# Attended values kept by feature, three score banks in turn, and the causal triangle added by VectorE in a fused attention and MoE kernel

## Chip, cores and metric

The kernel runs on one core of a Trainium2 chip. The metric is device time in microseconds for one execution. TensorE is the matrix engine (PE in the rows), VectorE is DVE, ScalarE is ACT, GpSimd is POOL, SyncE is SP.

## What is computed

```
xn  = layernorm(x)                       # x: 2 x 1024 x 512, float32
Q, K, V = xn @ Wq.T, xn @ Wk.T, xn @ Wv.T   # 16 heads of 32 features
S   = where(causal, Q K^T / sqrt(32), -1e30)
O   = softmax(S) @ V
att = O.reshape(b, t, D) @ Wo.T
ffn = sum over the top 2 of 8 experts (grouped sigmoid routing) of w * expert(xn)
      + shared(xn)                       # both are silu(x g^T) * (x u^T) d^T
out = x + att + ffn
```

Every large product is made in pieces: an operand is split into a rounded part (`_hi`) and a remainder (`_lo`), and the products of the parts are summed, so that float32 accuracy is kept with the fast `fp32r` matmul.

## The kernel before

Five phases follow each other, with a barrier between: norm, project (Q, K), attend, out (the Wo product and the residual), routed (the experts). The change touches attend and out.

**Attend.** 32 heads (16 heads by 2 batches), each in 12 steps; a step is one block of up to 128 keys by 512 queries. All five engines walk the same list of steps, each in its own order, and every stage has a lag in steps. On TensorE, in step s: `score(s-24)` (L1458), the piece of a second product for `maximum(s)` (L1432) that finds each row's maximum two heads ahead, `value(s-30)` (two matmuls, L1481 and L1483, that sum the 66 by 512 output of a head's half in `ps_o`), and between them `shared(s)`: so many matmuls of the shared expert (L1514, L1539) as the planner `fill_counts` gives that step. There are 864 of those, spread so that each step has the same planned cost (`step_cost`). Eight of a head's twelve blocks lie on the diagonal; there `score` adds the triangle of -1e30 with one more matmul, identity by `late` (L1463). Twice in a head `turn_o` turns the 66 by 512 output into rows with four transposes (L1494), after ScalarE has copied it (`o_copy`, L1252).

VectorE: `maximum` reduces each piece from one of two banks (L1306, L1310; L1314 joins two halves), `lo` for two of twelve blocks, `normalize` copies the turned output from PSUM (L1336), `weigh_o` takes the reciprocals of 128x4 sums (L1350), adds the two halves (L1352) and multiplies (L1356). The shared expert's `gate`, `hidden`, `hidden_lo` and `add` run on it too. ScalarE: `exp` from the score bank into one of four `prob` slots (L1236), then `hi` (L1243), the copies and the tanh. GpSimd: `lo` for ten of twelve blocks (L1198), and in between the steps of `place`, the list of routed rows, which ends in 32 indirect DMAs (L1166), one in each step. The order is copy, exp, row, hi on ScalarE. `ps_s` has two banks; `ps_x` is a bank shared by the turned output and by the turned row of maxima. SP issues loads head by head: six loads of Q and K, the values, and, at set heads, `load_xt`, `load_base`, `store_acc` and the raw weights of the second shared expert (`load_gate_up`, L1019), which ScalarE splits in `split_shared` (L1277).

**Out.** For each of 16 row tiles: VectorE copies the tile (L1651), TensorE turns it with four transposes (L1684), ScalarE and VectorE split it (L1636, L1657), TensorE multiplies by Wo in 12 matmuls (L1697), VectorE adds (L1665).

Of the kernel before, what the change touches and what calls it, by code (L numbers as in the profile page):

```python
# [33 lines left out]
P = 128  # L34
# [15 lines left out]
HEAD_SLOTS = 4  # L50
W_SLOTS = 4
# [39 lines left out]
def moe_attention_kernel(nc, x, wqk, wv, wo, router, bias, gate, up, down, sgate, sup, sdown, out):  # L91
# [5 lines left out]
    slots_dram = nc.dram_tensor("slots", [NSLOT, 2], F32, kind="Internal").ap()  # L97
    xt_dram = nc.dram_tensor("xt_blocks", [NTB, P, 2, KC, TBW], F32, kind="Internal").ap()
    with ExitStack() as ctx:
# [29 lines left out]
        with ExitStack() as shared_ctx:  # L129
# [25 lines left out]
            attend_phase(nc, x, ident, qk_hi, qk_lo, qs, ks, head_loaded, v_dram, row_dram, xt_dram,  # L155
# [25 lines left out]

def load_head(eng, g, qk_hi, qk_lo, qs, ks, head_loaded):

    c, h, b = g % HEAD_SLOTS, g // B, g % B
# [9 lines left out]
def wait_head_stored(eng, g, qk_stored):  # L194
    h, n = g // B, len(qk_stored)
# [583 lines left out]
def attend_phase(nc, x, ident, qk_hi, qk_lo, qs, ks, head_loaded, v_dram, row_dram, xt_dram, xt,  # L779
# [22 lines left out]
    COPY, TURN, NORM = VALUE + 1, VALUE + 2, VALUE + 3  # L802
    ROW = NB + 2
    DEEPEST = NORM
# [26 lines left out]
    def step_cost(s):  # L831
# [37 lines left out]

    def head_after(step):  # L870
        return max(0, -(-(step - (AHEAD + NB - 1) + 1) // NB) + HS)

    XT_AT = [None] + [head_after(step_of(unit - 1, UP_END[-1] - 1)) for unit in range(1, UNITS)]
    ACC_AT = [1] + [head_after(step_of(unit - 1, PER_UNIT - 1) + 1) for unit in range(1, UNITS)]
    RAW_AT = [2] + [head_after(min(SPLIT_AT, key=lambda s: SPLIT_AT[s] != [k - 1]) + 1)
                    for k in range(1, NF)]
    DOWN_RAW_AT = [3, 4, 5]

    with ExitStack() as ctx:
        sbuf, psum, sem = allocator(nc, ctx)  # L880
        vs = sbuf("vs", [P, HS, QT, VW], F32R)
        late = sbuf("late", [P, P], F32R)
        eye = sbuf("eye", [P, P], F32R)
# [9 lines left out]
        o_part = sbuf("o_part", [P, 4, VW])  # L893
        o_sum = sbuf("o_sum", [P, 4, DK])
        o_inv = sbuf("o_inv", [P, 4, 1])
# [17 lines left out]
        slot = sbuf("slot", [P, NT, E])  # L913
        pick = sbuf("pick", [P, NT, E])
# [4 lines left out]
        NS = 2  # L919
        ps_s = [psum(f"ps_s{n}", [P, TBW]) for n in range(NS)]  # L920
        ps_o = psum("ps_o", [P, TBW])
        ps_x = psum("ps_x", [P, TBW])
        ps_ot = ps_x[:, 0:4 * VW].rearrange("p (q w) -> p q w", q=4)
        ps_row = ps_x[:, TBW - P:]
        ps_f = [psum(f"ps_f{n}", [P, TBW]) for n in range(2)]

        values_loaded = [sem(f"values_loaded{n}") for n in range(HS)]
# [9 lines left out]
        s_done = sem("s_done")  # L937
        exp_done = sem("exp_done")
# [5 lines left out]
        o_turned = sem("o_turned")  # L944
        o_read = sem("o_read")
# [31 lines left out]
        with nc.Block() as block:  # L977
            @block.sync
            def _(sp):
# [6 lines left out]
                def load_values(g):  # L986
                    c, h, b = g % HS, g // B, g % B
                    wait(sp, pv_done, NB * (g - HS + 1))
                    sp.dma_start(vs[:, c, :, 0:2 * DK].bitcast(F32),
                                 v_dram[:, b * QT:(b + 1) * QT, h, :]).then_inc(values_loaded[c], 16)  # L990

# [34 lines left out]
                for g in range(HEADS + 4):  # L1026
                    if HS <= g < HEADS:
                        next_head(g)
                    if g == HEADS // 2:
# [4 lines left out]
                    for unit in range(UNITS):  # L1034
                        if g == XT_AT[unit]:
                            load_xt(unit)
                        if unit and g == ACC_AT[unit]:
                            store_acc(unit - 1)
                        if g == ACC_AT[unit]:
                            load_base(unit)  # L1040
                    if 0 < g <= HEADS:
                        load_values(g - 1)
                    for k in range(NF):
                        if g == RAW_AT[k]:
                            load_gate_up(k)
                        if g == DOWN_RAW_AT[k]:
                            load_shared_down(k)
                store_acc(UNITS - 1)
# [4 lines left out]
            def _(pool):  # L1053
# [23 lines left out]
                def place():  # L1077
# [86 lines left out]
                    for t in range(NT):  # L1164
                        for k in range(2):
# [14 lines left out]
                scratch = prob[:, 0, 0:P]  # L1180
                nc.gpsimd.memset(scratch, 0.0).then_inc(consts_zeroed, 1)
                pool.wait_ge(consts_zeroed, 2)
                nc.gpsimd.affine_select(out=scratch, in_=scratch, compare_op=ALU.is_ge,
                                        fill=MASKED, base=0, pattern=[[1, P]],
                                        channel_multiplier=-1).then_inc(consts_zeroed, 1)
                pool.wait_ge(consts_zeroed, 3)
                nc.gpsimd.tensor_copy(late[:, :], scratch).then_inc(consts_ready, 1)
                nc.gpsimd.tensor_copy(eye[:, :], ident[:, :]).then_inc(consts_ready, 1)
# [107 lines left out]
            def _(dve):  # L1296
# [32 lines left out]
                def normalize(s):  # L1329
                    if s % NB not in ENDS:  # L1330
                        return
# [643 lines left out]
```

## Time and profile before

| what | us |
|---|---|
| median of three runs (lowest, highest) | 1119.6 (1117.81, 1122.33) |
| the profiled execution's own time | 1127.01 |
| its span, first to last instruction | 1125.0 |
| norm and project | 0 to 184 |
| attend | 184 to 760.5 |
| out | 760.5 to 820.5 |
| routed | 820.5 to 1125 |
| busy, share of the span: TensorE, VectorE, ScalarE, GpSimd | 93%, 70%, 57%, 45% |
| VectorE's four operations on the turned output (L1336, L1350, L1352, L1356), busy in all | 27.1 + 10.8 + 41.1 + 33.2 = 112.2 |

A busy figure is an average over stages with different limits. The clock column is the TensorE clock granted, 1.00 for full speed (2.4 GHz), 0.5 for half (1.2 GHz). Matmuls are pipelined: a 512-column matmul is shown with some 0.4 us, while the next may start 0.23 us after it, so the distance between two starts is the cost, not the duration.

### The profile page before, as it was taken

The numbers are of one execution on the slowest core, as the hardware profiler recorded it, in microseconds if no ns is written. First come the engines' busy times: TensorE is split into PE (matmuls) and PEld (weight loads), VectorE is DVE, ScalarE is ACT, GpSimd is POOL, SyncE is SP. The second block draws the span as 40 slices with busy tenths as digits, with TensorE's granted clock in tenths as the row PEclk, the third lists the DMA queues.
The fourth block names the chain that finished last, engine by engine and source line by source line (L and its number), as shares of the span: only waits on it lengthen the run. The fifth ranks groups of instructions, "written<-read, shape, count | busy, mean of one in ns | idle before, by whom it ended". The sixth has DMA issues, their size and how long they took to land. (4 is left out here: it accounts for less than half of the span.)

```text
span 1125.0 us, 18890 instructions
## 1 busy us (share of the span) xinstructions
PE 1046.2 (93%) x5379; PEld 817.6 (73%) x5380; DVE 784.6 (70%) x1675; ACT 637.9 (57%) x1278; POOL 506.4 (45%) x568
## 2 busy tenths in 40 slices
PE   6999979888899998999999999998989999999994
PEld 4767867666677776777778777776867777778872
DVE  6732324565688887788888888865568888888872
ACT  3323211265588786787787887872155555565550
POOL 0013903388756564556566565651013443333321
PEclk9999989988899999999999999998989999999997
DMA  6989996255543553644445426118789444443432
GB/s 213 322 335 361 136 293 231 94 67 102 132 133 77 150 148 75 163 118 136 115 113 151 126 64 191 45 39 266 243 283 278 90 76 75 75 72 68 71 54 35
DMA packets 106201, 163.61 MB, mean 145 GB/s; under 512 B 53984, under 2 KB 64480, under 8 KB 102656
## 3 DMA queue, kind: packets, MB, share of 16 engines
q1 hardware_dynamic: 95776, 141.82, 44.1%
q0 software_dynamic: 9760, 20.49, 10.0%
q8 instruction: 38, 0.62, 0.2%
q14 instruction: 51, 0.42, 0.1%
q10 hardware_dynamic: 576, 0.26, 0.1%
HBM read 101.25 MB, written 61.28 MB: 144 GB/s over the span
## 5 line engine op out<-in xcount | busy, mean ns | idle before, releaser
L1198 POOL TENSOR_TENSOR prob_lo<-prob,prob_hi 128x512 fp32r<-128x512 f32 (+2 forms) x320 | 308.3, 977 | 203.3 <-ACT prob_hi L1243 147.0
L1236 ACT ACTIVATE prob<-ps_s 128x512 f32<-128x512 f32 (+3 forms) x384 | 188.0, 490 | 127.1 <-PE ps_s L1463 77.1
L1243 ACT ACTIVATE prob_hi<-prob 128x512 fp32r<-128x512 f32 (+3 forms) x384 | 198.6, 517 | 12.4 <-ACT row_stage L1217 12.4
L1862 DVE TENSOR_TENSOR rw_lo<-gu_sb,rw_hi 128x704 fp32r<-128x704 f32 x156 | 138.8, 893 | 52.7 <-ACT rw_hi L1806 47.7
L1306 DVE CUSTOM_DVE_ANT_0 ps_m<-ps_m,causal 128x384 f32<-128x384 f32 (+3 forms) x256 | 126.7, 495 | 69.2 <-PE ps_m L1432 66.9
L1806 ACT ACTIVATE rw_hi<-gu_sb 128x704 fp32r x156 | 123.5, 794 | 62.8 <-PE ps_ru L1895 43.6
L1458 PE MATMUL ps_s<-qs,ks 97*128 97x512 f32 (+3 forms) x384 | 140.4, 366 | 9.4 <-ACT prob L1236 9.2
L1779 POOL DMA_INDIRECT out<-work,slot_table x39 | 63.5, 1627 | 181.1 <-DVE work L1847 148.2
L1481 PE MATMUL ps_o<-prob_hi,vs 128*66 128x512 f32 (+3 forms) x384 | 133.1, 347 | 10.4 <-issue 9.6
L1432 PE MATMUL ps_m<-ks,qs 96*128 96x512 f32 (+3 forms) x384 | 139.1, 362 | 0.6 <-DVE maxima L1306 0.2
L1483 PE MATMUL ps_o<-prob_lo,vs 128*66 128x512 f32 (+3 forms) x384 | 132.0, 344 | 0.0
L1310 DVE TENSOR_REDUCE maxima<-ps_m 128x1 f32<-128x512 f32 x128 | 85.8, 682 | 41.5 <-PE ps_m L1432 40.4
L1916 PE MATMUL ps_ry<-d_sb,work 128*128 (+1 forms) x234 | 106.9, 593 | 1.2 <-issue 1.2
L1458 PEld LDWEIGHTS ps_s<-qs,ks 97*128 97x128 f32 x384 | 74.8, 195 | 30.8 <-ACT prob L1236 15.9
L1432 PEld LDWEIGHTS ps_m<-ks,qs 96*128 96x128 f32 x384 | 74.3, 193 | 23.6 <-DVE maxima L1306 4.6
L613 PE MATMUL ps_q<-xt,w_hi 128*128 128x512 f32 x256 | 82.0, 398 | 6.4 <-DVE work L725 6.4
L1481 PEld LDWEIGHTS ps_o<-prob_hi,vs 128*66 128x66 f32 x384 | 54.3, 141 | 32.1 <-issue 21.4
L725 DVE TENSOR_TENSOR work<-ps_q,work 128x512 fp32r<-128x512 f32 x32 | 21.8, 690 | 78.8 <-ACT work L574 76.9
L1514 PE MATMUL ps_f<-xt,sg_hi 128*128 128x512 f32 (+1 forms) x192 | 70.5, 400 | 3.8 <-PEq L496 2.7
L1514 PE MATMUL ps_f<-xt,su_hi 128*128 128x512 f32 (+1 forms) x192 | 71.5, 406 | 0.0
L1916 PEld LDWEIGHTS ps_ry<-d_sb,work 128*128 128x128 f32 (+1 forms) x234 | 43.4, 190 | 38.7 <-issue 38.7
L1768 POOL DMA_INDIRECT work<-xn_rows,slot_table x35 | 37.5, 1073 | 58.8 <-PE ps_xt L1883 48.7
(201 smaller groups left out, 2353.0 us busy)
## 6 DMA issues: line engine op xcount, KB each, us to landing
xt<-xt_blocks SPq DMA_DIRECT2D x7, 2048.0 KB, 9.1
v_rows<-work SPq DMA_DIRECT2D x16, 512.0 KB, 3.0
xt_blocks<-xt SPq DMA_DIRECT2D x4, 2048.0 KB, 11.3
qk_hi<-work SPq DMA_DIRECT2D x8, 1024.0 KB, 4.7
qk_lo<-work SPq DMA_DIRECT2D x8, 1024.0 KB, 7.5
qs<-qk_hi SPq DMA_DIRECT2D x64, 128.0 KB, 2.9
ks<-qk_hi SPq DMA_DIRECT2D x64, 128.0 KB, 3.2
vs<-v_rows SPq DMA_DIRECT2D x32, 256.0 KB, 4.7
```

The lines of the kernel that those rows point to most:

```text
L1198: nc.gpsimd.tensor_tensor(prob_lo[:, s % NPL, 0:w], prob[:, s % NP, 0:w], prob_hi[:, s % NPH, 0:w].bitcast(F32), ALU.subtract).then_inc(lo ...
L1236: nc.scalar.activation(prob[:, s % NP, 0:w], ps_s[s % NS][:, 0:w], ACT.Exp, scale=SCALE).then_inc(exp_done, 1)
L1243: nc.scalar.activation(prob_hi[:, s % NPH, 0:w], prob[:, s % NP, 0:w], ACT.Copy).then_inc(hi_ready, 1)
L1306: nc.vector.tensor_tensor_reduce(ps_m[s % NM][:, 0:w], ps_m[s % NM][:, 0:w], causal[:, TBW - w:], 1.0, MASKED, ALU.add, ALU.max, maxima[:, ...
L1432: nc.tensor.matmul(ps_m[s % NM][:, 0:w], qs[0:ROWS, c, t * P:(t + 1) * P], ks[0:ROWS, c, k0:k0 + w], start=True, stop=True).then_inc(m_don ...
L1458: last = nc.tensor.matmul(ps_s[s % NS][:, 0:w], ks[0:ROWS + 1, c, kt * P:(kt + 1) * P], qs[0:ROWS + 1, c, q0:q0 + w], start=True, stop=not ...
L1481: nc.tensor.matmul(into, vs[:, c, kt, :], prob_hi[:, s % NPH, 0:w], start=n in STARTS, stop=False)
L1483: nc.tensor.matmul(into, vs[:, c, kt, :], prob_lo[:, s % NPL, 0:w], start=False, stop=n in ENDS).then_inc(pv_done, 1)
L1514: last = nc.tensor.matmul(ps_f[part][0:w, :], (w_hi, w_lo, w_hi)[term][:, kc, f0:f0 + w], xt[:, (0, 0, 1)[term], kc, :], start=(j == 0), s ...
L1806: nc.scalar.activation(w_hi[:, k, :], chunk(e, k), ACT.Copy).then_inc(w_hi_ready, 1)
L1862: nc.vector.tensor_tensor(w_lo[:, k, :], chunk(e, k), w_hi[:, k, :].bitcast(F32), ALU.subtract).then_inc(w_lo_ready, 1)
L1916: last = nc.tensor.matmul(ps_y[c % 2][:, :], hid_t[0:w, c % HR, k, :], d_sb[0:w, bass.ds(e * NF + k, 1), :].rearrange("p a d -> p (a d)"), ...
```

## The change

1. **Attended values by feature.** `turn_o`, the copy from PSUM, and the per-half reciprocal, sum and product go. Instead SP moves the copied 66 by 512 output with DMAs: 32 features of the first part into `attended` at partitions 32n, 32 of the second into `o_low`, and the row of sums to DRAM (`place_output`, two steps after the last value step); two steps later `spread_sums` waits for that store and loads the row back over 32 partitions of `o_den`. Four heads of one batch fill 128 partitions; heads are taken in that order (`head_of`). When the fourth is placed, VectorE does one sum, one reciprocal and one product over 128x512, for each half: 16 sets in all.
2. **Three banks in turn.** `ps_x` goes; scores and turned rows of maxima share three banks (`bank`, `wait_bank_read`). ScalarE does `hi` before `exp`.
3. **The triangle.** VectorE adds `late` to 128 columns of the score bank (`mask`, 256 of them), and `exp` waits for it on diagonal blocks.
4. **SP and the planner.** SP's list is by steps, not heads; two value slots, not four; `load_gate_up` and others are placed by step. `step_cost` drops the 60 of the triangle and the 270 of the turns, and gives each of the first 24 steps at least 520.
5. **Out.** The tiles are already by feature: the copy and the four transposes of each tile go, and the split reads SBUF.

```diff
+def head_of(g):
+    return QUAD * (g // (QUAD * B)) + g % QUAD, g // QUAD % B
...
-            cost += span(n)[1] / 2.25 + (60 if n in DIAGONAL else 0)
+            cost += span(n)[1] / 2.25
...
-        if 0 <= s - TURN < STEPS and (s - TURN) % NB in ENDS:
-            cost += 270
+        if s < AHEAD:
+            cost = max(cost, 520)
...
+    RAW_AT = {NB: 0, **{s + 2: ks[0] + 1 for s, ks in SPLIT_AT.items() if ks[0] + 1 < NF}}
...
-        NS = 2
+        NS = 3
...
+                def place_output(s):
...
+                    sp.wait_ge(o_copied, 2 * g + half + 1)
+                    if n == 0:
+                        wait(sp, o_ready, 2 * (g // QUAD - 1) + half + 1)
...
+                        sp.dma_start(into, o_copy[rows, half, :].rearrange("p (a q) -> p a q", a=4)
+                                     ).then_inc(o_placed[half], 16)
...
+                    sp.dma_start(den_dram[o:o + 1, :], o_copy[2 * DK:2 * DK + 1, half, :]
+                                 ).then_inc(den_saved, 16)
+                def spread_sums(s):
...
+                    sp.wait_ge(den_saved, 16 * (o + 1))
+                    sp.dma_start(o_den[n * DK:(n + 1) * DK, half].rearrange("p a q -> p (a q)"),
+                                 den_dram[o:o + 1, :].broadcast_to([DK, TBW])
+                                 ).then_inc(o_placed[half], 16)
...
+                    if s % NB in DIAGONAL:
+                        act.wait_ge(masked, count(DIAGONAL, s))
...
-                    for lag, stage in ((COPY, copy_o), (EXP, exp), (ROW + 1, row), (HI, hi),
+                    for lag, stage in ((COPY, copy_o), (HI, hi), (EXP, exp), (ROW + 1, row),
...
+                def mask(s):
+                    if s % NB in DIAGONAL:
+                        dve.wait_ge(s_done, s + 1)
+                        nc.vector.tensor_tensor(bank("score", s)[:, 0:P], bank("score", s)[:, 0:P],
+                                                late[:, :], ALU.add).then_inc(masked, 1)
...
+                def sum_outputs(s):
...
+                    dve.wait_ge(o_placed[half], 48 * (g + 1))
+                    nc.vector.tensor_tensor(of, of, o_low[:, half], ALU.add).then_inc(normalizing, 1)
+                    nc.vector.reciprocal(o_den[:, half], o_den[:, half]).then_inc(normalizing, 1)
...
+                    nc.vector.tensor_tensor(of, of, o_den[:, half], ALU.mult).then_inc(o_ready, 1)
...
+                    for lag, stage in ((AHEAD, mask), (0, maximum), (LO, lo), (NORM, sum_outputs),
+                                       (NORM + 1, normalize)):
...
-                    if diagonal:
-                        last = nc.tensor.matmul(ps_s[s % NS][:, 0:P], eye[:, :], late[:, :],
-                                                start=False, stop=True)
...
-                    for q in range(4):
-                        last = nc.tensor.transpose(ps_ot[:, q, 0:VW], o_copy[:, o % 2, q * P:(q + 1) * P],
-                                                   ident[0:VW, 0:VW])
...
-                    for k in range(KC):
-                        last = nc.tensor.transpose(ps_t[c % R][:, k, :], a_tile[:, c % R, k * P:(k + 1) * P],
-                                                   ident[:, :])
```

## Rows read from the trace of the kernel before

**Rows 1.** Busy time of each engine by stretch, us.

```profile
core 0: us, PE busy (x) PEld busy (x) DVE busy (x) ACT busy (x) POOL busy (x), PEclk, DMA share, GB/s
184.00:219.00 35.00, 31.53 (x132) 23.98 (x131) 20.80 (x51) 5.24 (x8) 17.23 (x57) 0.95 0.56 179
...
229.00:296.00 67.00, 55.87 (x252) 39.14 (x251) 40.06 (x98) 35.35 (x81) 60.36 (x60) 0.83 0.65 118
...
424.00:428.00 4.00, 2.03 (x9) 0.97 (x8) 2.93 (x7) 3.35 (x8) 0.46 (x1) 0.94 0.02 6
428.00:432.00 4.00, 4.00 (x17) 3.16 (x18) 1.90 (x3) 1.93 (x5) 1.81 (x2) 0.64 0.00 0
444.00:448.00 4.00, 1.25 (x6) 0.70 (x6) 2.22 (x7) 2.68 (x7) 0.00 (x0) 1.00 0.01 4
...
500.00:724.00 224.00, 221.49 (x1255) 174.30 (x1254) 189.43 (x486) 178.56 (x405) 137.18 (x143) 1.00 0.43 120
```

**Rows 2.** Timeline of ScalarE, one row copy a head: start us, duration us.

```profile
310.52 0.25 ACT L1217 ACTIVATE row_stage<-ps_x 8x128 fp32r<-8x128 f32 x1
...
421.42 0.25 ACT L1217 ACTIVATE row_stage<-ps_x 8x128 fp32r<-8x128 f32 x1
440.81 0.25 ACT L1217 ACTIVATE row_stage<-ps_x 8x128 fp32r<-8x128 f32 x1
460.64 0.25 ACT L1217 ACTIVATE row_stage<-ps_x 8x128 fp32r<-8x128 f32 x1
...
587.61 0.25 ACT L1217 ACTIVATE row_stage<-ps_x 8x128 fp32r<-8x128 f32 x1
602.77 0.25 ACT L1217 ACTIVATE row_stage<-ps_x 8x128 fp32r<-8x128 f32 x1
...
728.60 0.25 ACT L1217 ACTIVATE row_stage<-ps_x 8x128 fp32r<-8x128 f32 x1
```

**Rows 3.** Timeline of TensorE's matmuls, 280 to 282 us, of attend.

```profile
280.85 0.23 PE L1463 MATMUL ps_s<-late,eye 128*128 128x128 f32 x1
280.91 0.28 PE L1481 MATMUL ps_o<-prob_hi,vs 128*66 128x256 f32 x1
...
281.62 0.41 PE L1494 MATMUL ps_x<-ident,o_copy 66*128 66x66 f32 x4
281.83 0.36 PE L1432 MATMUL ps_m<-ks,qs 96*128 96x256 f32 x1
```

**Rows 4.** GpSimd's indirect DMAs in 229 to 296 us: busy, mean ns, idle before.

```profile
L1166 POOL DMA_INDIRECT slots<-entry,slot_of x32 | 33.5, 1046 | 6.0 <-issue 5.4 <-PE ps_o L1483 0.6
```

**Rows 5.** Timeline of ScalarE at 445 us; in brackets its idle time and what ended it.

```profile
445.32 0.52 ACT L1277 ACTIVATE sg_hi<-gu_raw 128x384 fp32r<-128x384 f32 x1 [1.80 <-DMA gu_raw<-in_sup]
```

**Rows 6.** VectorE's groups by shape in attend: busy us, mean ns, idle before.

```profile
L1310 DVE TENSOR_REDUCE maxima<-ps_m 128x1 f32<-128x512 f32 x128 | 85.8, 682 | 41.5 <-PE ps_m L1432 40.4
...
L1306 DVE CUSTOM_DVE_ANT_0 ps_m<-ps_m,causal 128x128 f32<-128x128 f32 x64 | 19.1, 298 | 28.2 <-PE ps_m L1432 28.1
```

**Rows 7.** VectorE's reciprocals by line: duration ns min/median/max, start us, shape.

```profile
L1350 DVE RECIPROCAL o_inv<-o_part x64: 158/171/181, 237.7 to 759.6; 128x4 f32<-128x4 f32 x64
L744 DVE RECIPROCAL total<-total x1: 254/254/254, 141.3 to 141.3; 128x16 f32<-128x16 f32 x1
```

**Rows 8.** Timeline of GpSimd just after 141 us: start us, duration us.

```profile
141.27 1.28 POOL L707 TENSOR_TENSOR sd_lo<-sd_raw,sd_hi 96x512 fp32r<-96x512 f32 x1
```

**Rows 9.** Timeline of all engines at the end of attend.

```profile
757.98 0.59 ACT L1252 ACTIVATE o_copy<-ps_o 66x512 f32<-66x512 f32 x1 [2.89 <-PE ps_o L1483]
...
760.55 0.82 SPq L1602 DMA_DIRECT2D d_sb<-in_wo  x2
```

**Rows 10.** DMA issues: size of one, median us from issue to landing.

```profile
qs<-qk_hi SPq DMA_DIRECT2D x64, 128.0 KB, 2.9
```

**Rows 11.** Timeline of TensorE in out, 793 to 795 us.

```profile
793.65 0.60 PE L1684 MATMUL ps_at<-ident,a_tile 128*128 128x128 f32 x4
794.01 0.48 PE L1697 MATMUL ps_ay<-wo_hi,a_hi 128*128 128x512 f32 x1
```

More of the change, by code:

```diff
@@ L50 @@
 HEAD_SLOTS = 4
+V_SLOTS = 2
+QUAD = P // DK
 W_SLOTS = 4
@@ L918, in attend_phase, with bank, wait_bank_read @@
         ps_m = [psum(f"ps_m{n}", [P, TBW]) for n in range(NM)]
-        NS = 2
+        NS = 3
         ps_s = [psum(f"ps_s{n}", [P, TBW]) for n in range(NS)]
+        uses = [use for s in range(ALL) for use in (
+            ([("score", s - AHEAD)] if 0 <= s - AHEAD < STEPS else [])
+            + ([("row", (s - ROW) // NB)] if 0 <= s - ROW < STEPS and (s - ROW) % NB == 0 else []))]
+        use_of = {use: n for n, use in enumerate(uses)}
+        def bank(*use):
+            return ps_s[use_of[use] % NS]
+        def wait_bank_read(eng, *use):
+            before = use_of[use] - NS
+            if before >= 0:
+                kind, n = uses[before]
+                eng.wait_ge(exp_done if kind == "score" else row_ready, n + 1)
         ps_o = psum("ps_o", [P, TBW])
-        ps_x = psum("ps_x", [P, TBW])
-        ps_ot = ps_x[:, 0:4 * VW].rearrange("p (q w) -> p q w", q=4)
-        ps_row = ps_x[:, TBW - P:]
         ps_f = [psum(f"ps_f{n}", [P, TBW]) for n in range(2)]
-        values_loaded = [sem(f"values_loaded{n}") for n in range(HS)]
+        values_loaded = [sem(f"values_loaded{n}") for n in range(V_SLOTS)]
         row_saved = sem("row_saved")
@@ L943, in attend_phase @@
         o_copied = sem("o_copied")
-        o_turned = sem("o_turned")
-        o_read = sem("o_read")
+        o_placed = [sem(f"o_placed{n}") for n in range(2)]
+        den_saved = sem("den_saved")
         normalizing = sem("normalizing")
@@ L1423, in _ @@
             def _(pe):
-                turned = {"rows": 0, "outputs": 0}
                 def maximum(s):
@@ L1440, in turn_row @@
                     pe.wait_ge(max_ready, g + 1)
-                    wait(pe, row_ready, g)
-                    wait(pe, o_read, turned["outputs"])
-                    nc.tensor.transpose(ps_row[0:QT, :], maxima[:, c, 0:QT],
+                    wait_bank_read(pe, "row", g)
+                    nc.tensor.transpose(bank("row", g)[0:QT, 0:P], maxima[:, c, 0:QT],
                                         ident[:, :]).then_inc(row_turned, 1)
-                    turned["rows"] += 1
                 def score(s):
@@ L1565, in _ @@
                         shared(s)
-                    for lag, stage in ((TURN, turn_o), (0, maximum), (ROW, turn_row)):
+                    for lag, stage in ((0, maximum), (ROW, turn_row)):
                         if 0 <= s - lag < STEPS:
@@ L1647, in _ @@
             def _(dve):
-                def copy(i, c):
-                    t = U * i + c
-                    wait(dve, turned, t - R + 1)
-                    nc.vector.tensor_copy(a_tile[:, c % R, :], attended[:, bass.ds(t, 1), :]
-                                          .rearrange("p a d -> p (a d)")).then_inc(tile_ready, 1)
                 def lo(i, c):
```

218 lines of the change are left out of this document (98 added, 120 removed).

## The prediction

> **What bounds the kernel now.** I read the busy table by stretch first, then the pace of the heads, then single timelines where the pace breaks. Attend has four stretches.
>
> (a) 184 to 219 us, the 24 steps before the first score: TensorE is busy for 31.5 of 35 us [rows 1], with 108 of the 864 shared matmuls placed there by the planner.
>
> (b) 229 to 296 us: GpSimd is busy for 60.4 of 67 us and the clock is 0.83 [rows 1]. Its 32 indirect DMAs of 1.05 us, plus 5.4 us of issue, stand between its `lo` steps [rows 4]. TensorE waits there, so work taken from TensorE buys nothing.
>
> (c) 296 us to the end: TensorE is busy for 221.5 of 224 us at clock 1.00, VectorE for 189.4, ScalarE for 178.6 [rows 1]. The best heads take 15.2 us (587.61 to 602.77) and I count a plain head at 15.45; from 310.52 to 728.60 it is 26 heads in 418.1 us, 16.1 each [rows 2]. Two heads took 19.4 and 19.8 us [rows 2]. In the second ScalarE stood for 1.8 us for the raw weights [rows 5] and TensorE was idle for 2.75 us (444 to 448); in the first it was idle for 1.97 us (424 to 428), and the clock of the next 4 us was 0.64 [rows 1]. So an idle time of 2.0 us cost 4.0, one of 2.75 us cost 4.4. This price is needed below.
>
> (d) The end of attend and out.
>
> **Part by part.** Sums are against the profiled execution (span 1125.0, its own time 1127.0; the median is 1119.6, 7.4 lower); the difference is then taken from the median.
>
> The triangle's matmul. From its start to the next is 0.06 us in [rows 3]; with what it adds to a neighbour of 128 columns I take 0.08. Eight in a head: -0.64 us. The turns: 0.21 us for four [rows 3], twice: -0.42. Following `fill_counts` with the new costs, the first 24 steps hold 65 shared matmuls, not 108, and the other heads some 24 each, not 22.8: +1.2 x 0.23 = +0.28. A plain head goes from 15.45 to 14.65. This counts from 296 us to the last value (757.6), 29.3 heads: -23 us. In (b) it is worth nothing.
>
> The raw weights. `load_gate_up` moves to two steps after the last split, some ten steps (12 us) before its use. The two long heads lose 3.9 and 4.4 us: -8. (Bounds 0 and -9.) The other loads moved by step keep several steps of lead; SP gets 4 DMAs a half, but a head of 12 steps leaves it time, and its waits are for things done a step or two before.
>
> The first 24 steps. 43 matmuls fewer, 43 x 0.23 = 9.9 us, and most of the 3.5 us without work go, since no unit of the shared expert must end in them: -13 (bounds -7 and -16). Row and load of the first head still fit. Stretch (b) then only starts earlier; GpSimd's work is the same.
>
> Out. From the start of the turns to the first product is 0.36 us [rows 11], and I take 0.44 with what they add behind them, as at the triangle: x 15 tiles = -7. The copy and the splits are hidden (TensorE is the pace). Loading of experts and tiles has to fit the shorter phase: bounds -7 and -3.
>
> Now what is added. The mask: 256 on VectorE. Nearest row: the 128-column operation on a PSUM bank and an SBUF tile, 298 ns [rows 6], 8 x 0.3 = 2.4 us a head. What goes with the turned output is more than that (112.2 us in the table above, 3.5 a head). A third bank gives the score one more step of time, so in plain steps I cost the new wait at 0 (bounds 0 and +0.8 us a head: VectorE has 35 of 224 us free in (c)). If VectorE is late, `exp` is, and then the score three steps on.
>
> **The reciprocal is the term that decides.** It was 128x4 and becomes 128x512, 16 times, in VectorE's order before the masks and maxima of the next steps. For 4 columns it takes 171 ns, for 16 columns 254 ns [rows 7]: 83 ns for 12 columns, 6.9 each. I don't put that down to waiting for GpSimd, because that engine's operation beside it ran from 141.27 to 142.55 us [rows 8] and the reciprocal, begun at 141.3 [rows 7], was done by 141.6. So 512 columns take 0.25 + 496 x 0.0069 = 3.7 us. From below, if it streams as a 512-column maximum does (682 ns [rows 6]): 0.7 us; from above, if 254 ns were all per column: 8 us. I take 3.7, nearest to the widest row. The Trainium skill, page "VectorE: DVE Perf Modes", section "First, the fixed hardware budget", says that Reciprocal iterates a divide with a repeat count of 8. At its 0.96 GHz that would be an estimate of 8.3 ns a column, 4.4 us; the sum would come out some 10 us higher. The trace's 6.9 is nearer to that than to one column a cycle.
>
> What does TensorE do in that time? VectorE has finished the maximum of the set's step 0.55 us after TensorE ended that step, then sum (0.7) and reciprocal (3.7) until 4.95, then the next maximum until 5.55. TensorE can run two more steps and the score and values of the third, since there are two `ps_m` banks: 3.4 us. It stands for 2.15 us. By the two gaps above, idle and slower clock after it, that is 4.1 us. 14 of the 16 sets fall before the last score (the two of the last quad don't): +57 us. For the first half's set the sums are also spread late: SP's six head loads stand between the store and the load back, and store and load take some 2.9 us each [rows 10]; I add 0.6 us for 7 sets: +4.
>
> The end. Before, 2.6 us from the copy's start to the first load of out [rows 9]. After: copy 0.6, three issues 1.2, store 2.9, issue and load 3.3, sum 0.7, reciprocal 3.7, product 0.7: 13.1 us, so +10 (bounds +6 and +15).
>
> Sum: -23 - 8 - 13 - 7 + 57 + 4 + 10 = +20 with every wait paid in full; some idle time that plain heads have now (15.45 against the best 15.2 [rows 2]) will fall into the same gaps, -0.1 us a head, -3: +17. The profiled time goes to 1144, the median to 1119.6 + 17 = 1137 us.
>
> **The rivals.**
> A, the reciprocal is quick: 0.7 us, a set is hidden in the 3.4 us that TensorE can go on. Then -51 for what goes and +7 for the end: -44, 1076 us. The 171 ns of 4 columns speak for it, the 254 ns against it.
> B, the gaps don't bring the clock down: 14 x 2.15 = 30 in place of 57, so -10: 1110 us. Against it stand the 0.64 behind a gap of 1.97 us [rows 1].
> C, slower still: VectorE has no time left. Masks, and sets whose reciprocal runs over 4.4 us, and the chain mask, `exp`, `hi`; from the point where mask and set need more than VectorE's free 35 of 224 us (2.4 us a head [rows 1]) a head stays at 15.45. It takes back 23 us and puts each gap at 5, 13 more: 1173 us.
> D, it doesn't do what it says: the turns only move to SP's queue, and `o_placed` becomes the wait for `copy_o`. Nine steps lie between; I give it little, and count it with C.
>
> **Chances.** Forecast 0.58, with 1118 to 1160 as its own range. A 0.17, B 0.10, C with D 0.15. A and B are faster, as is a small part of the forecast: 0.28. Within 0.5% (5.6 us, about what a measurement of this kernel can tell from no change) lies the lower edge of the forecast and the upper of B: 0.13. Slower: 0.59. The range takes in A's middle and nearly C's, 1073 to 1170; what lies beyond either is some 2 in 10.
>
> **What would show it.** The 128x512 reciprocal's row: 3.5 us or more, and behind it a maximum whose TensorE wait is 2 us, 14 times, with a clock under 1.00 in the 4 us after. Between the sets heads of 14.6 us; the first score at some 206 us, not 219; no 19 us heads at the raw weights; out in 53 us; from the last copy to out 13 us. A row of 0.7 us for the reciprocal would make the prediction wrong at once; so would rows of 3.7 us with TensorE going on behind them, which would mean that the slack is longer than 3.4 us.

## The result, and the profile after

| | before | after |
|---|---|---|
| median of the runs side by side, us | 1120.44 (1117.81 to 1122.33) | 1224.94 (1220.28 to 1229.87) |
| ratio, 95% interval | | 1.0935 (1.0881 to 1.0989) |
| the profiled execution's span, us | 1125.0 | 1220.6 |
| mean granted clock | 0.97 | 0.94 |

The changed kernel is 104 us slower. The forecast was 1137 us with a range to 1170: right in sign, far off in size. The spans differ by 95.6 us, and the timelines of the two split it like this (us):

| stretch | before | after | difference | forecast |
|---|---|---|---|---|
| start of attend (no line of it changed) | 184.3 | 180.3 | -3.9 | 0 |
| from there to the first score | 34.6 | 20.4 | -14.2 | -13 |
| first score to the row copy of the sixth head, GpSimd's stretch | 91.6 | 92.1 | +0.5 | 0 |
| 26 heads, row copy to row copy | 418.1 | 531.2 | +113.1 | together |
| from there to the last copy of ps_o | 29.4 | 27.6 | -1.8 | +27 |
| that copy to out's first load | 2.6 | 10.3 | +7.7 | +10 |
| out | 60.0 | 55.7 | -4.3 | -7 |
| routed | 304.5 | 303.0 | -1.5 | 0 |

The forecast for the heads and for the stretch behind them was one sum, +27 against a measured +111.3. So only that sum is wrong by much, and it is wrong by 84 us. (One execution of the run e11 below took 3806 us, where its three others took 1108 to 1114; it is left out of that run's figures.) The pace of the heads after, to be held against [rows 2] (same view, one row copy a head):

```profile
565.26 0.25 ACT L1268 ACTIVATE row_stage<-ps_s 8x128 fp32r<-8x128 f32 x1
584.96 0.25 ACT L1268 ACTIVATE row_stage<-ps_s 8x128 fp32r<-8x128 f32 x1
601.71 0.25 ACT L1268 ACTIVATE row_stage<-ps_s 8x128 fp32r<-8x128 f32 x1
618.43 0.25 ACT L1268 ACTIVATE row_stage<-ps_s 8x128 fp32r<-8x128 f32 x1
644.37 0.25 ACT L1268 ACTIVATE row_stage<-ps_s 8x128 fp32r<-8x128 f32 x1
```

The head with two reciprocals takes 25.9 us, the one behind it 19.7, a plain head 16.7, where the forecast had some 23, 14.65 and 14.65. The busy table by stretch, against [rows 1]:

```profile
core 0: us, PE busy (x) PEld busy (x) DVE busy (x) ACT busy (x) POOL busy (x), PEclk, DMA share, GB/s
...
500.00:724.00 224.00, 180.16 (x810) 132.06 (x808) 166.64 (x396) 142.72 (x316) 108.20 (x112) 0.91 0.45 121
454.00:458.00 4.00, 1.75 (x9) 1.01 (x7) 3.49 (x2) 0.94 (x2) 0.69 (x2) 1.00 0.29 66
458.00:462.00 4.00, 0.00 (x0) 0.00 (x0) 3.56 (x9) 1.50 (x4) 0.00 (x0) 0.77 0.00 0
462.00:466.00 4.00, 2.98 (x9) 2.31 (x10) 1.56 (x4) 2.33 (x5) 1.31 (x2) 0.50 0.14 33
```

From 500 to 724 us TensorE is busy for 180 us, not 221, at clock 0.91; and no other engine is full (VectorE 167 of 224). Work stands in a chain, not in front of an engine that is full over the whole stretch. VectorE's groups by shape (busy, mean ns, idle before) and the waits of ScalarE and TensorE (us in total, times, longest):

```profile
L1401 DVE RECIPROCAL o_den<-o_den 128x512 f32<-128x512 f32 x16 | 53.5, 3342 | 0.0
L1375 DVE TENSOR_TENSOR ps_s<-ps_s,late 128x128 f32<-128x128 f32 x256 | 76.6, 300 | 5.6 <-PE ps_s L1503 5.4
```

```profile
ACT prob L1290 <- DVE ps_s L1375: 175.0, 113, 7.4
PE ps_o L1524 <- issue: 56.0, 26, 7.7
PE ps_o L1524 <- ACT o_copy L1306: 36.0, 27, 2.9
PE ps_m L1482 <- DVE maxima L1364: 17.4, 7, 3.0
```

Both new operations last as long as was forecast (3.34 us against 3.7, 300 ns against 298). But `exp` waits 175 us for masks, where before it waited 98 us in all for score matmuls (77.1 and 21.0), and TensorE's greatest wait is not the one the prediction worked with (`ps_m`, 17 us). It is 92 us at `ps_o`, of which the profile gives 36 to `o_copy` and leaves 56 as "issue". The 56 are the same wait: with the copy moved one step earlier (e5, below) 1.9 of them are left, and of the 36 there are 9.1. The timeline at one of the longest, 7.3 us, shows how it comes about (without weight loads, SP's queue and GpSimd; in brackets idle time and what ended it):

```profile
455.17 3.34 DVE L1401 RECIPROCAL o_den<-o_den 128x512 f32<-128x512 f32 x1
455.35 0.40 PE L1544 MATMUL ps_f<-xt,sg_hi 128*96 128x512 f32 x1
458.43 0.62 DVE L1428 SCALAR_TENSOR_TENSOR hid<-gated,ps_f 128x512 f32<-128x512 f32 x1
458.97 0.68 DVE L1360 CUSTOM_DVE_ANT_0 ps_m<-ps_m,causal 128x512 f32<-128x512 f32 x1
...
459.58 0.68 DVE L1410 TENSOR_TENSOR work<-work,o_den 128x512 f32<-128x512 f32 x1
460.18 0.28 DVE L1375 TENSOR_TENSOR ps_s<-ps_s,late 128x128 f32<-128x128 f32 x1
...
460.50 0.38 ACT L1290 ACTIVATE prob<-ps_s 128x256 f32<-128x256 f32 x1 [5.52 <-DVE ps_s L1375]
460.78 0.62 ACT L1322 ACTIVATE hid_hi<-hid 128x512 fp32r<-128x512 f32 x1
461.30 0.62 ACT L1331 ACTIVATE sg_hi<-gu_raw 128x512 fp32r<-128x512 f32 x1
461.82 0.62 ACT L1331 ACTIVATE su_hi<-gu_raw 128x512 fp32r<-128x512 f32 x1
462.34 0.58 ACT L1306 ACTIVATE o_copy<-ps_o 66x512 f32<-66x512 f32 x1
...
463.01 0.66 PE L1524 MATMUL ps_o<-prob_hi,vs 128*66 128x512 f32 x1 [7.26 <-issue]
```

Read it from the bottom. The values of a new half can't start before the half before has been copied out of the one `ps_o` bank. The half had ended at some 454.6 us, but `copy_o` stands on ScalarE a step later, behind the `exp` of the step before. That `exp` waits for its mask, the mask for VectorE, and VectorE is in the reciprocal and then in the `hid`, the maximum and the product that stand between it and the mask. This is also a head with raw weights: `hid_hi` and two splits of ScalarE, 1.6 us, stand between `exp` and the copy. The 4 us with TensorE at zero are followed by 4 us at 0.50, half of 2.4 GHz. In each of the seven heads with two sets TensorE stood like this at the first set, for 4.8 to 7.7 us. At the second it stood for 2.6 to 3.0 us at `ps_m`, where the prediction had looked for it, in six of the seven; in the other for 3.5 us for a sum of the shared expert. The rest of the 92 us, some 50, falls outside the sets.

### The profile page after: what moved, and what is told of

Its sections match the earlier page's. It is cut to its first block and busy times, and to the rows that moved or that the text cites. A ratio compares the mean times of both kernels' runs of the same rounds, so it can differ in the third digit from the quotient of the medians.

```text
span 1220.6 us, 17825 instructions
## 1 busy us (share of the span) xinstructions
PE 1035.6 (85%) x4803; PEld 783.0 (64%) x4804; DVE 816.2 (67%) x1707; ACT 649.2 (53%) x1278; POOL 507.1 (42%) x566
## 5 line engine op out<-in xcount | busy, mean ns | idle before, releaser
L1249 POOL TENSOR_TENSOR prob_lo<-prob,prob_hi 128x512 fp32r<-128x512 f32 (+2 forms) x320 | 312.7, 990 | 297.0 <-PE ps_o L1526 192.3
L1524 PE MATMUL ps_o<-prob_hi,vs 128*66 128x512 f32 (+3 forms) x384 | 140.3, 366 | 93.2 <-issue 56.0
L1297 ACT ACTIVATE prob_hi<-prob 128x512 fp32r<-128x512 f32 (+3 forms) x384 | 200.9, 523 | 27.6 <-ACT row_stage L1268 11.3
L1482 PE MATMUL ps_m<-ks,qs 96*128 96x512 f32 (+3 forms) x384 | 141.8, 369 | 18.7 <-DVE maxima L1364 17.4
L1503 PE MATMUL ps_s<-qs,ks 97*128 97x512 f32 (+3 forms) x384 | 144.2, 376 | 10.5 <-ACT prob L1290 7.2
L1526 PE MATMUL ps_o<-prob_lo,vs 128*66 128x512 f32 (+3 forms) x384 | 136.7, 356 | 0.0
L1482 PEld LDWEIGHTS ps_m<-ks,qs 96*128 96x128 f32 x384 | 78.4, 204 | 50.9 <-DVE maxima L1364 20.9
L1503 PEld LDWEIGHTS ps_s<-qs,ks 97*128 97x128 f32 x384 | 78.4, 204 | 38.7 <-ACT prob L1290 16.7
L1375 DVE TENSOR_TENSOR ps_s<-ps_s,late 128x128 f32<-128x128 f32 x256 | 76.6, 300 | 5.6 <-PE ps_s L1503 5.4
L1544 PE MATMUL ps_f<-xt,sg_hi 128*128 128x512 f32 (+1 forms) x192 | 75.0, 426 | 2.7 <-PEq L504 2.7
L1385 DVE TENSOR_TENSOR prob_lo<-prob,prob_hi 128x512 fp32r<-128x512 f32 x64 | 69.2, 1081 | 0.4 <-ACT prob_hi L1297 0.4
```

Source lines behind the costliest of these rows:

```text
L1249: nc.gpsimd.tensor_tensor(prob_lo[:, s % NPL, 0:w], prob[:, s % NP, 0:w], prob_hi[:, s % NPH, 0:w].bitcast(F32), ALU.subtract).then_inc(lo ...
L1297: nc.scalar.activation(prob_hi[:, s % NPH, 0:w], prob[:, s % NP, 0:w], ACT.Copy).then_inc(hi_ready, 1)
L1482: nc.tensor.matmul(ps_m[s % NM][:, 0:w], qs[0:ROWS, c, t * P:(t + 1) * P], ks[0:ROWS, c, k0:k0 + w], start=True, stop=True).then_inc(m_don ...
L1503: nc.tensor.matmul(bank("score", s)[:, 0:w], ks[0:ROWS + 1, c, kt * P:(kt + 1) * P], qs[0:ROWS + 1, c, q0:q0 + w], start=True, stop=True). ...
L1524: nc.tensor.matmul(into, vs[:, c, kt, :], prob_hi[:, s % NPH, 0:w], start=n in STARTS, stop=False)
L1526: nc.tensor.matmul(into, vs[:, c, kt, :], prob_lo[:, s % NPL, 0:w], start=False, stop=n in ENDS).then_inc(pv_done, 1)
```

## The experiments

Times are medians beside a median of before of 1122.0 (e1 to e4), 1123.1 (e5 to e8), 1122.0 (e9 to e12) and 1123.6 (f1 to f4). Times of heads are distances between two row copies in the one profiled execution of a run. A plain head is one without a set, not next behind one, and without a split of raw weights. The cuts of code are shortened; comments in them are mine.

### Reciprocal and mask apart: e1, e2, e3

e1, reciprocal over 4 columns:

```diff
-nc.vector.reciprocal(o_den[:, half], o_den[:, half])
+nc.vector.reciprocal(o_den[:, half, :, 0:1], o_den[:, half, :, 0:1])
```

> The changed kernel, but the reciprocal runs over 4 columns of the sums and not over 512 (the rest of the normalisation is left out: outputs are not normalised). Theory T: after a set VectorE is late by 3.3 us, the mask, the exp and the copy of ps_o behind it (ScalarE works in order) are late by that, and TensorE stands at the start of a half's values, which needs the copy; a head with two sets takes 25.6 to 29.2 us and the one behind it 18.5 to 20.7, against 16.2 to 17.8 of the others, so some 10 + 2 us for each of 7 heads: 1225 - 85 = 1140 us, the heads 24, 28 ... like the others. Rival R1, VectorE has no time to spare in the whole: only its own 53 us come back at the most, 1172 us or more. Rival R2, what stalls the fourth heads is the placing by DMA and the sum that waits for it (o_placed, 6.7 us in all), not the reciprocal: 1215 us or more. Rival R3, the mask has the greater part: 1190 us or more.

Measured 1166.6 us, ratio 1.038 (1.032 to 1.044). The outputs of this kernel, of e3 and of e8 are not normalised; the instructions are otherwise the same.

e2, the triangle by the matmul as before, the wide reciprocal stays:

```diff
-nc.vector.tensor_tensor(bank("score", s)[:, 0:P], bank("score", s)[:, 0:P], late, ALU.add)
+nc.tensor.matmul(bank("score", s)[:, 0:P], eye, late, start=False, stop=True)
```

> The changed kernel, but the triangle is added by the matmul as before (eye times late, and 60 in the planner's cost), no mask on VectorE; the order hi before exp, three banks and the wide reciprocal stay. Theory T: the mask is in the chain of every diagonal step, plain heads of 16.2 to 17.8 us go back to 14.7 or 15.2 (some -2 us in each of 29 heads, -55), and the set's reciprocal no longer stands ahead of an exp, so its heads lose more than that: 1225 - 55 - 30 = 1140 us, with the set's heads at 20 us. Rival R4, the plain heads are slow for the order hi before exp or for GpSimd's lo beside VectorE, not for the mask: plain heads stay at 16.5 and the time at 1200 us or more. Rival R1 (VectorE's time only): 256 x 0.3 = 77 us less work on VectorE, at most -77 and no smaller gap at the sets.

Measured 1166.2 us, ratio 1.036 (1.030 to 1.043). The planner's 60 for the triangle comes back with the matmul, here and in the other kernels with it.

> Both edits: reciprocal over 4 columns (not normalised) and the triangle by the matmul. Theory T: nothing is left of the chain but the late maximum; plain heads of 14.9 us, all heads alike, 1075 us. Rival R2 (placing by DMA): every fourth head still long, 1120 us. Rival R4 (order of hi and exp, three banks): plain heads of 16.5, 1130 us.

Measured 1105.1 us, ratio 0.982 (0.977 to 0.988).

The two costs add up: from the sixth row copy to the last, 26 heads take 531.2 us in the changed kernel, 474.9 without the wide reciprocal, 473.7 without the mask, 416.5 without both. The reciprocal costs 57.3 us (473.73 - 416.46), the mask 58.4 us (474.85 - 416.46), together 114.7. The waits for the copy of `ps_o` go with the mask: 92 us in the changed kernel, 72 in e1 (mask, 4 columns), 23.5 in e2, 13.4 in e3. All three of my sizes for e1 to e3 were off by 25 to 30 us: in e1 and e2 I had expected either repair to mend part of the other, and in e3 plain heads took 15.0 to 15.5 us and not 14.9, and four heads (three with splits of raw weights) 18.5 to 19.6. Rival R2 (transfers are the cause) falls with e3. R1 (VectorE's own time) has its bound of 1172 us crossed by e1, but by 5 us only: the 58 us of e1 are near VectorE's 53. It takes e5 to part them.

### Where the copy stands: e5, f2

```diff
-for lag, stage in ((COPY, copy_o), (HI, hi), (EXP, exp), ...
+for lag, stage in ((HI, hi), (VALUE, copy_o), (EXP, exp), ...
```

VALUE is one less than COPY: the copy is made in the step of the half's last value, ahead of that step's `exp`.

> The changed kernel with one thing moved: ScalarE copies ps_o in the step in which the half's last value runs, ahead of that step's exp, and not in the next step behind it. Mask and wide reciprocal stay. Theory T: a plain head (16.2 to 17.8 us in the changed kernel) is long because the copy stands behind an exp that waits for its mask, so that TensorE stands twice a head for 1 us at the first value of a half; with the copy ahead of that exp plain heads take 15.2 to 15.7 us and the time is 1225 - 30 = 1195 us, or 1185 if the sets' heads gain too. Rival R5, the mask's cost is in the probabilities' own chain (mask, exp, hi, lo, value) and not in the copy: plain heads stay at 16.5 us or more, 1215 us or more. Rival R1 (VectorE's time only): no change, 1220 to 1230.

Measured 1174.7 us, ratio 1.041 (1.034 to 1.048): 50 us less for the place of one instruction in an order, more than I had expected. The waits for the copy of `ps_o` fall from 92 to 11 us. Plain heads range from 14.5 to 15.5 us, where the changed kernel had 16.2 to 17.8; these two have 14.8 and 14.7:

```profile
558.65 0.25 ACT L1268 ACTIVATE row_stage<-ps_s 8x128 fp32r<-8x128 f32 x1
573.47 0.25 ACT L1268 ACTIVATE row_stage<-ps_s 8x128 fp32r<-8x128 f32 x1
588.19 0.25 ACT L1268 ACTIVATE row_stage<-ps_s 8x128 fp32r<-8x128 f32 x1
```

R1 falls: VectorE does the same work here. The same edit on e2 (no mask, wide reciprocal):

> The kernel with the triangle by the matmul (1166 us, wide reciprocal in one piece after the spread) and ps_o copied ahead of exp. Tells where a set's price comes from. Theory T: the first half's set made TensorE stand 4.9 us at the first value of a half, since the copy stood on ScalarE behind a hid_hi that waited for VectorE; with the copy ahead only the wait for a ps_m bank is left, 2.0 us as the prediction had it (plus what o_den's transfer keeps VectorE waiting), the sets' heads fall from 24.4 to 20.5 and the time by 7 x 4 + what the copy brings elsewhere, to 1135 us. Rival R7: the chain of the probabilities is late by itself, and the place of the copy only moves the wait: 1155 us or more.

Measured 1151.6 us, ratio 1.025 (1.020 to 1.029). From 300 us on no wait for `ps_o` is left, and what is left is the wait of the prediction, for `ps_m`. TensorE's waits from 300 to 760 us, and the two sets of one head (first half at 579, second at 594.5):

```profile
PE ps_m L1484 <- DVE maxima L1362: 22.5, 10, 3.8
PE ps_m L1484 <- DVE maxima L1366: 16.9, 7, 2.8
```

```profile
578.00:580.00 2.00, 1.02 (x5) 0.39 (x3) 2.00 (x2) 0.34 (x2) 0.00 (x0) 1.00 0.68 157
580.00:582.00 2.00, 0.00 (x0) 0.00 (x0) 2.00 (x3) 0.04 (x1) 0.00 (x0) 1.00 0.18 45
582.00:584.00 2.00, 1.36 (x7) 1.23 (x8) 2.00 (x6) 1.97 (x5) 0.76 (x1) 0.95 0.10 33
584.00:586.00 2.00, 2.00 (x7) 1.50 (x6) 2.00 (x4) 0.95 (x3) 1.43 (x2) 0.50 0.00 0
586.00:588.00 2.00, 2.00 (x11) 1.77 (x10) 1.12 (x4) 1.86 (x4) 0.88 (x1) 0.70 0.01 2
...
594.00:596.00 2.00, 0.47 (x3) 0.03 (x1) 2.00 (x2) 0.60 (x2) 1.63 (x2) 1.00 0.37 76
596.00:598.00 2.00, 1.58 (x9) 1.30 (x10) 2.00 (x5) 0.42 (x2) 0.59 (x1) 0.86 0.00 0
598.00:600.00 2.00, 2.00 (x6) 1.26 (x6) 1.24 (x4) 0.91 (x2) 0.41 (x1) 0.50 0.01 2
600.00:602.00 2.00, 2.00 (x10) 1.52 (x9) 0.89 (x3) 0.99 (x2) 0.46 (x1) 0.79 0.01 4
```

TensorE stands for 3.6 us at the first set and 1.9 at the second; in e2, with the late copy, it stood for 4.9 and 2.0. The second is the prediction's case (2.15). By the clock column TensorE then ran at half speed for some 3.4 us behind each gap (0.2 + 2.0 + 1.2 and 0.6 + 2.0 + 0.8), which loses 1.7 us each. At the first, VectorE had waited 1.07 us for the spread sums, and a `hid` of the shared expert (0.63 us) lies between reciprocal and maximum. A quad of heads takes 68.8 us (295.55 to 364.39) against four plain ones at 14.95, 59.8: 9.0 us for two sets, which is 3.6 + 1.9 us of gaps and 2 x 1.7 for the clock. I had expected 1135, and the sets' heads fell only to 21 to 24 us, not 20.5. Theory T had held for the head at 594 us in e2, but not for all: of the seven first sets in e2 only three stood at `ps_o` (3.5, 5.5 and 4.9 us), the others at `ps_m` (2.1 to 4.4). In f2 the first sets stand at `ps_m` for 1.9 to 3.8 us. So the greater part of those three gaps only moved, as R7 has it, though the time is 3 us below R7's 1155.

### One long absence or several short ones: e6, e12

```diff
-nc.vector.reciprocal(o_den[:, half], o_den[:, half])
...
+nc.vector.reciprocal(o_den[:, half, q], o_den[:, half, q])   # q = 0..3, in steps NORM + q
```

> The kernel with the triangle by the matmul (1166 us), and the same reciprocal done in four pieces of 128 columns in four following steps instead of one of 512; the product comes three steps later. VectorE's work is the same. Theory T: what costs is how long VectorE is away at once (3.3 us against 0.8 us); the heads with sets go from 24.4 us and 16.2 behind them to some 17.5, the time to 1166 - 50 = 1115 us. Rival R1 (VectorE's time in all, or its stretch beside GpSimd): 1160 to 1170 us. Rival R2 (the sets are long for o_den's wait on DMA): 1155 us.

Measured 1125.6 us, ratio 1.0015 (0.9985 to 1.0045), 41 us less than e2 and 10 more than expected, although the pieces cost VectorE more than the whole:

```profile
L1409 DVE RECIPROCAL o_den<-o_den 128x128 f32<-128x128 f32 x64 | 59.5, 938 | 0.0
```

The same with mask and early copy:

> The changed kernel, mask and spreading of sums as they are, with two repairs in the order alone: ps_o copied ahead of exp, and the 128x512 reciprocal in four pieces of 128 columns in four steps. VectorE's work is the same or a little more (4 x 0.94 us in place of 3.34). Theory T: the early copy alone gave 1175 us; the pieces give back most of what the sets cost (23 to 27 us heads to 17 or 18): 1175 - 45 = 1130 us. Rival R1 (VectorE's time in all, with the masks): 1160 us or more.

Measured 1147.4 us, ratio 1.022 (1.017 to 1.028): 27 us less than e5, not 45. The heads with sets still take 21 to 25 us. A mask, a maximum and a piece of 0.94 us are more than a step of 1.2 us, and VectorE is busy for 21.2 us of such a head of 22.4 (361.1 to 383.6 us). So VectorE's own time most likely counts over the steps of a set, as R1 says; no run parts that from the rest.

### Inverting before spreading: e7, e9, e10

The sums of four heads are loaded as 128x16, inverted, stored and then spread.

```diff
+sp.dma_start(o_few[:, half], rows_of(den_dram, o)) ...            # VALUE + 4
...
+sp.dma_start(rows_of(inv_dram, 2 * g + half), o_few[:, half]) ... # VALUE + 8, spread at + 10
...
+nc.vector.reciprocal(o_few[:, half], o_few[:, half]) ...          # VALUE + 7
...
-nc.vector.reciprocal(o_den[:, half], o_den[:, half])
```

> The kernel with the triangle by the matmul (1166 us), and the reciprocal taken before the sums are spread: four heads' 2048 sums are loaded as 128x16, inverted, stored, and only then spread over the rows of a head; all is computed. Theory T: a set costs VectorE 0.25 us and not 3.34, so the heads are as with 4 columns, 15.2 to 15.9 us, and the time is that of the kernel with 4 columns and the matmul (1105 us) plus 4 to 6 us for two more transfers at the end: 1110 us. Rival R2 (waits on transfers, of which there are now more and in SP's queue ahead of the head loads): 1140 us or more.

Measured 1138.2 us, ratio 1.011 (1.005 to 1.018), 28 us more than expected. This kernel takes the sum at VALUE + 13 and the product a step later. R2 has its case here, made by me: VectorE stood for the transfers.

```profile
DVE work L1441 <- DMA o_den<-inverses: 21.7, 10, 6.6
```

So in the next two the sum is taken early (VALUE + 6) and the product 14 steps after it; both have the early copy. They differ in the triangle alone, with the planner's 60 for it.

> The changed kernel (VectorE's mask, three banks) with ps_o copied ahead of exp and the sums inverted as 128x16 before they are spread; sum and product apart, the product 14 steps after the sum, so that VectorE doesn't wait for transfers. Theory T: no long absence of VectorE is left and the copy doesn't stand behind a masked exp, so a plain head is 14.7 us, a head with sets some 16, and three heads with raw weights 19: 1095 us. Rival R5 (VectorE with mask, maxima, lo and the shared expert's part is too full to follow 14.7 us heads): plain heads of 15.5 us or more, 1120 us. Rival R2 (transfers): 1130 us or more, with VectorE's waits on o_den again in the tens of us.

> The same as the run beside it (copy ahead of exp, 128x16 inverses, late product), but with the triangle by the matmul. The difference of the two is the mask alone, once nothing waits behind it. Prediction's terms: 0.55 to 0.64 us a head of TensorE's time, so this one 15 us longer than the other where TensorE is the bound: 1110 us. If VectorE is too full (R5), this one is the faster of the two.

e9, with the mask: 1115.4 us, ratio 0.994 (0.991 to 0.997). e10, with the matmul: 1091.8 us, ratio 0.9735 (0.971 to 0.977). The sign is the opposite of what I had expected, and R5 is nearer for e9 (1120 us), though plain heads stay under its 15.5: the mask costs 1.1 us a head more than the matmul (26 heads in 423.1 us against 394.9). The profiled execution of e10 is its fastest, 1082.4 us where the others took 1090.6 to 1093.8; but f1 below, profiled at 1089.5, has the same plain heads. With the wide reciprocal the price is the same: 483.1 us in e5, 455.9 in f2, again 1.0 a head. The busy table of both over 15 heads or so (e10 first, then e9):

```profile
456.00:681.00 225.00, 224.08 (x1219) 180.13 (x1219) 167.19 (x413) 195.40 (x429) 159.52 (x151) 1.00 0.56 155
```

```profile
480.00:705.00 225.00, 214.82 (x1052) 159.20 (x1051) 181.12 (x512) 186.52 (x412) 142.87 (x145) 1.00 0.55 153
```

With the matmul TensorE is busy for 224 of 225 us, a plain head takes 14.9 us and a head with sets 15.6. With the mask the plain heads in which VectorE has no `hid` of the shared expert are quicker (14.4 to 14.7) and those in which it has one are slower (15.1 to 15.4); heads with sets take 16.0 to 18.8, those next behind them 15.1 to 16.5, and those with raw weights 19.0 to 21.1.

### The order of hi and exp: e8

On e3, exp ahead of hi as before.

> The kernel with the triangle by the matmul and the reciprocal over 4 columns (1105 us, not normalised), with ScalarE's order as in the kernel before: exp, then row, then hi. Theory T: without a mask exp waits for nothing from VectorE, TensorE is busy nearly all of the time and the order is worth nothing: 1100 to 1110 us. Rival R4 (the order itself stretches the operations on VectorE that run beside GpSimd, prob_lo 1166 ns against 786 before): prob_lo falls to 0.8 us and the time to 1095 or less.

Measured 1111.3 us, ratio 0.988 (0.983 to 0.993). VectorE's `prob_lo` falls as R4 has it, and nothing comes of it:

```profile
L1387 DVE TENSOR_TENSOR prob_lo<-prob,prob_hi 128x512 fp32r<-128x512 f32 x64 | 49.4, 773 | 1.4 <-ACT prob_hi L1299 1.3
```

In e3 the mean of this group is 1166 ns. 6 us between the two medians the other way are within what two kernels' starts differ by (below), and the 26 heads take 417.4 us against 416.5.

### The mask in the kernel before: e4, f3, f4

> The kernel before with the triangle added in PSUM by VectorE alone (two score banks, exp before hi, outputs turned by TensorE as before; 60 less in the planner's cost). Prediction's step (a mask hidden in plain steps): -5 us, 1115 us. Theory T: the mask delays the exp of eight of twelve steps by VectorE's queue, and with two banks sooner the score: plain heads from 15.5 to 17 or more, 1165 us or more. Rival R4: within 10 us of before.

Measured 1229.5 us, ratio 1.096 (1.089 to 1.103). The triangle's way alone, with nothing else of the change but the planner's 60, costs 107 us. With the early copy:

> The kernel before with VectorE's mask (1229 us) and ps_o copied ahead of that step's exp. If the copy behind the masked exp is the greater part of the mask's price there too: 1229 - 50 = 1180 us. If with two score banks the score itself waits for the late exp (PE ps_s waited 54 us there, ps_o 61): it falls by less than 30 us, 1200 or more.

1188.2 us, ratio 1.059 (1.053 to 1.064): 41 us less, as the first line of it had it. What is left is the wait for a score bank, of which there are two:

```profile
PE ps_s L1462 <- ACT prob L1235: 68.0, 76, 2.2
```

> The kernel before with ps_o copied ahead of that step's exp, nothing else. Theory T: without a mask nothing keeps exp waiting, TensorE is busy for 221 of 224 us from 500 to 724, so at most the 10 us of waits for ps_o in the whole kernel are there to be had: 1112 to 1122 us.

1112.0 us, ratio 0.9885 (0.984 to 0.993): the early copy is a gain of 12 us in the kernel before too, at the lower edge of what I had expected. Between f3 and f4 the mask costs 76 us even with the early copy; the 28 us between e9 and e10 are with three banks.

### The heads with raw weights: e11, f1

```diff
-for k in SPLIT_AT.get(s, ()):
...
-    for n, w_hi in enumerate((sg_hi, su_hi)):   # two of 128x512 in one step
...
+for m in range(4):
+    for k in SPLIT_AT.get(s - m, ()):           # four of 128x256 in four steps
```

> The kernel with mask, early copy and 128x16 inverses, and the three splits of the raw gate and up weights (two of 128x512 on ScalarE and on VectorE in one step, three times) made in four pieces of half the size in four following steps; their loads four steps later. Theory T: the three heads of 18 to 19.5 us are long because VectorE is away for 2.2 us at once, twice 0.7 to 1.5 us behind its prob_lo; in pieces they fall to 16, and the time by 3 x 3 = 9 us, to 1086. Rival R6, those heads are long for the loads of the raw weights: no change against the kernel without it.

1109.2 us, ratio 0.990 (0.985 to 0.995), 6 us less than e9 in the medians; the three heads take 15.8, 17.2 and 18.0 us instead of 19.0, 19.9 and 21.1, 9.0 us less.

> The fastest so far (triangle by the matmul, ps_o copied ahead of exp, 128x16 inverses, late product: 1092 us) and the raw gate and up weights split in four pieces in four steps. Theory T: the three heads of 16.7 us that are left fall to 15.2, 1092 - 5 = 1087 us. If they are long for the loads (R6): 1092.

1090.0 us, ratio 0.969 (0.965 to 0.974). The three heads go from 16.7 each to 15.2, 15.2 and 16.1, 3.6 us less; the median moves by 2. In both kernels the heads get shorter, though the loads come later still, so it is the splits, and R6 falls. Of the totals the difference can't be told from none. This is the fastest kernel of the study, 3% below the one before.

## Why the prediction was wrong, point by point

**The size of the reciprocal: right.** 3.34 us against 3.7. The two shapes put the rate at (3342 - 254) / 496 = 6.2 ns a column, against 6.9 from [rows 7]; the 8.3 that I estimated from the Trainium skill, "VectorE: DVE Perf Modes", section "First, the fixed hardware budget", is too high, though its sentence on an iterated divide points the right way. Rival A is out.

**The price of a set: right in sum, wrong in its path.** 57 us was forecast, plus 4 and less 3; e1 to e3 give 57.3. By f2 a pair of sets costs 9.0 us where only `ps_m` is waited for, against 2 x 4.1 + 0.6 = 8.8. But in the changed kernel TensorE waits at `ps_o` at the first set of each head, for 4.8 to 7.7 us and not 2.15. In e1, with 4 columns, it stands there for 1.8 to 4.5 us behind the mask alone, so the wide reciprocal adds some 3 us (2.7 to 3.6). The slack of 3.4 us counted `ps_m` and score banks, and not the single `ps_o` bank whose copy stands behind `exp` on an in-order engine; and it counted no `hid` ahead of the next maximum. That the sum came out within 1 us is in part luck. Rival B (no price for the clock) is out: the 5.5 us of idle time of f2 cost 9.0, with the clock at 0.50 behind both gaps.

**The mask: this is the step that failed.** It was set at 0 (bounds 0 and 0.8 us a head) because VectorE had 35 of 224 us free and a third bank gave the score a step more of time. Both are true and neither is the question. The mask stands between score and `exp`, `exp` stands ahead of `copy_o`, and the next half's first value stands behind that; twice a head, 1 us each. 58 us in 26 heads is 2.2 a head, and the gain of TensorE's time, 0.64 a head, was booked on top. Together (58 and 29.3 x 0.64 = 19) that is 77 of the 84 us by which the heads are off, and the raw weights' 8 (below) are about the rest. The place of the copy is shown as the cause of half of it: with the early copy the mask costs 27 us over the 26 heads (e5 against f2) or 28 (e9 against e10), in place of 58. The other half is a price of the mask too, and how it comes about stays open (below). Rival C had the chain (mask, `exp`, `hi`) but let a plain head stay at 15.45; it took 16.7, and C with its 1173 us was some 50 short too.

**The matmul's removal: too large, and not to be had.** The 14.7 us of e5's quickest heads meet the forecast's 14.65 by luck: the early copy, which the forecast did not have, is in them. With early copy and matmul a plain head takes 14.9 us (f2, e10), with the mask at best 14.4 to 14.7, so in the heads where nothing waits the matmul is worth 0.2 to 0.5 us and not 0.64. And over a whole row of heads the mask is 1.1 us a head dearer than the matmul (e9, e10) even then.

**The raw weights: wrong.** -8 was booked for two heads that waited for a load. After the change the three heads with splits took 19.2, 29.0 (this one with two sets) and 20.7 us, and in e3, without mask and sets, 19.5, 19.4 and 18.5. The wait for the load [rows 5] is gone from the profile, and the splits set the length: made in smaller pieces they take less (e11, f1). A stall went, and what was late next was not looked for.

**The first 24 steps: right.** -14.2 against -13. **Out**: -4.3 against -7, within the bounds of -7 and -3. **The end**: +7.7 against +10; the store of the sums took 1.4 us there from its issue to the next one (853.54 to 854.92) and the load back 2.0 (to the sum at 856.94), not 2.9 and 3.3. **GpSimd's stretch**: 24.2 and 24.7 us a head as before, as said.

**Rival D**: `copy_o` never waited for `o_placed` in the profile's rows. VectorE did wait for spread sums, 6.7 us in all.

What stays open: by which path the mask costs its remaining 1.1 us a head. From e10 to e9 TensorE's waits for the copy of `ps_o` grow from 1.0 to 15.2 us, early copy or not, those for `ps_m` from 4.8 to 7.8 and those for a score bank from 7.7 to 11.1, which is some 21 of the 28; how they divide between VectorE's queue and ScalarE's no run shows. Two starts of attend in kernels that share all code before it lie up to 9 us apart (177.1 in e10, 186.5 in f2), so differences of a few us between two of these kernels are not explained here.

## What to carry to other kernels

Before an operation is moved to an engine with free time, write down what stands behind its consumer in that consumer's in-order queue, and which single buffer waits for that: half of the price was there, and none of it in the busy shares. A copy that frees a single buffer belongs ahead of anything in its queue that can be made to wait: in the four kernels where it was moved alone it gave 50, 15, 41 and 12 us (e5, f2, f3, f4). And what counts for an engine that feeds others is its longest absence against the buffers' slack: the same reciprocal cost 41 us less in four pieces (without the mask), and, over 16 columns before the spreading, nearly nothing once its transfers had steps enough (e10: a head with two sets takes at most 0.7 us more than a plain one).

## What the runs showed of the hardware

A VectorE reciprocal costs 254 ns for 128x16, 938 for 128x128 (e6) and 3342 for 128x512, where adding two 128x512 tiles takes 0.69 us (f2, at 577.4 us). Behind a gap of 3.6 us without a matmul the granted clock was 0.50 of 2.4 GHz, that is 1.2 GHz, for some 3.4 us, and behind one of 1.9 us as well (f2), so each of these gaps cost its own length and some 1.7 us more, the short one as much as the long one. `prob_lo` on VectorE, with both inputs in SBUF, took 1166 ns when ScalarE's order let it start together with GpSimd's, and 773 when not (e3, e8): 0.68 us with GpSimd's `prob_lo` not beside it, up to 1.8 us with it. The mask, with one input in PSUM, took 296 to 300 ns in every kernel that has it. The Trainium skill, "SBUF — State Buffer", section "Who interferes with whom", says that a VectorE instruction contends with GpSimd's reads when both its inputs are in SBUF; the traces agree. Here that stretch moved no median that could be told from none (e3, e8).
